# Causal mask of a 16-head attention layer: one full-height product a tile in place of two of half height

## The reference

```python
Q = (x @ Wq + bq).reshape(B, S, 16, 16)      # K, V alike
logits = jnp.einsum('bqhd,bkhd->bhqk', Q, K) * scale
causal = jnp.tril(jnp.ones((S, S), bool))
attn = jax.nn.softmax(jnp.where(causal, logits, -jnp.inf), axis=-1)
gated = attn * gate[:, None, None, :]        # gate: a small net on x
out = jnp.einsum('bhqk,bkhd->bqhd', gated, V).reshape(B, S, E) @ Wo + bo
```

## Time and profile before

| | us |
|---|---|
| median of 3 runs (3470.48 to 3481.04) | 3470.54 |
| the profiled execution | 3475.61 |
| its span, first to last instruction | 3473.8 |
| PE busy | 3212.1 (92%) |
| DVE busy | 1895.7 (55%) |
| ACT busy | 1481.7 (43%) |
| mean granted clock of PE | 0.964 |

### The profile page before, as it was taken

One profiled execution on the slowest core, in us unless ns is written; L12 is line 12 of the kernel. 1 busy time (PEld: TensorE's weight loads), 2 busy tenths in 40 slices (PEclk: granted clock), 3 DMA queues, 4 the chain that ended last, 5 costly groups with the idle time before them and its releaser, 6 DMA issues. The chain is left out here.

```text
span 3473.8 us, 50032 instructions
## 1 busy us (share of the span) xinstructions
PE 3212.1 (92%) x18306; PEld 2318.3 (67%) x18306; DVE 1895.7 (55%) x3245; ACT 1481.7 (43%) x2723; POOL 912.6 (26%) x818
## 2 busy tenths in 40 slices
PE   7996999999999999999998798998999889999998
PEld 4665756976578755986577545556465468888887
DVE  4544744775466743876465575756657433333332
ACT  3331254423543144423543465464755544444443
POOL 1213413753256512753256101001010011111111
PEclk9997999999999999999999899999999999999999
DMA  5111111111111111111111100010000130000000
GB/s 195 64 43 56 37 27 45 37 49 33 30 47 54 41 27 41 45 49 30 30 50 48 27 2 26 2 21 6 2 25 2 36 150 13 13 13 13 7 7 13
DMA packets 184276, 126.20 MB, mean 36 GB/s; under 512 B 125281, under 2 KB 164449, under 8 KB 180577
## 3 DMA queue, kind: packets, MB, share of 16 engines
q1 hardware_dynamic: 184032, 122.97, 12.4%
HBM read 105.47 MB, written 28.44 MB: 39 GB/s over the span
## 5 line engine op out<-in xcount | busy, mean ns | idle before, releaser
L1655 ACT ACTIVATE l3b_prob<-sums 128x512 f32<-128x512 f32 (+3 forms) x768 | 333.1, 494 | 204.9 <-PE sums L1588 165.8
L1904 PE MATMUL sums<-l_uhi,l_h 128*128 128x512 f32 x1024 | 405.9, 396 | 0.0
L1904 PE MATMUL sums<-l_ulo,l_h 128*128 128x512 f32 x1024 | 405.3, 396 | 0.0
L685 POOL TENSOR_TENSOR l_qrow<-l_vm,l_qst 128x512 fp32r<-128x512 f32 x256 | 355.0, 1401 | 167.8 <-ACT l_qst L679 148.9
L1025 DVE TENSOR_REDUCE l2b_mx<-sums 128x1 fp32r<-128x1024 f32 (+7 forms) x256 | 192.7, 758 | 269.4 <-PE sums L937 267.6
L962 PE MATMUL sums<-sb_nx,l_vx 128*128 128x512 f32 (+3 forms) x768 | 307.3, 510 | 2.1 <-ACT l_od L1000 2.1
L993 ACT ACTIVATE sb_nx<-sums 128x512 f32<-128x512 f32 (+3 forms) x384 | 183.7, 493 | 263.1 <-PE sums L954 257.9
L1583 PE MATMUL sums<-l_qst,l_kst 64*128 64x512 f32 (+3 forms) x768 | 277.8, 426 | 18.0 <-DMA l_qst<-l3b_peak 8.8
L1990 DVE TENSOR_TENSOR l_ulo<-l_made,l_uhi 128x512 fp32r<-128x512 f32 x128 | 90.5, 707 | 362.1 <-ACT l_uhi L1921 362.0
L679 ACT CAST l_qst<-l_vm 128x512 fp32r<-128x512 f32 x256 | 157.8, 620 | 238.2 <-DVE l_vm L672 223.6
L1566 PE MATMUL sums<-l_kst,l_qst 64*128 64x512 f32 (+3 forms) x768 | 236.9, 431 | 20.8 <-DVE l3b_low L1667 10.9
(11 more groups left out here) (273 smaller groups left out, 7806.2 us busy)
## 6 DMA issues: line engine op xcount, KB each, us to landing
l_ve<-ve SPq DMA_DIRECT2D x34, 512.0 KB, 4.0
l_oe<-oe SPq DMA_DIRECT2D x16, 1024.0 KB, 6.5
l_vm<-weights_copy SPq DMA_DIRECT2D x32, 352.0 KB, 3.3
sb_nx<-between SPq DMA_DIRECT2D x9, 1024.0 KB, 5.7
weights_copy<-h SPq DMA_DIRECT2D x2, 4096.0 KB, 25.4
l_ve<-inverse SPq DMA_DIRECT2D x32, 256.0 KB, 3.6
l_qst<-l3b_peak SPq DMA_DIRECT2D x512, 0.5 KB, 2.0
l_h<-weights_copy SPq DMA_DIRECT2D x2, 4096.0 KB, 23.4
```

Of the source, the lines that this page charges most:

```text
L685: pool.tensor_tensor(rlo[:, i % RT, :], routed[:, i % RT, :], rhi[:, i % RT, :].bitcast(F32), ALU.subtract).then_inc(s3.routed_lo, 1)
L1655: act.activation(prob[:, i % RB, j, a, 0:hi - lo], bank(m.ps, part % SCORE, 0, hi - lo), ACT.Exp, scale=SCALE1).then_inc(s.exp_ready, 1)
L1904: run(lambda out, a, x, first, last: pe.matmul(out, a, x, start=first, stop=last))
```

## The change

The two products of 64 rows that add the mask to a tile become one product of 128 rows and 128 columns, the bf16 identity times the whole mask, for maxima and score tiles alike. The constants `rowpick` and `rowmask`, their two loads and their three casts on ScalarE go, and the wait for the loads counts 14 in place of 16.

```diff
-HPART = P // 2
...
-    rowpick = sb("rowpick", [P, 2, P], BF16)
-    rowmask_qk, rowmask_kq = sb("rowmask_qk", [P, 2, P], BF16), sb("rowmask_kq", [P, 2, P], BF16)
...
-                     (w1, "w13"), (hv, "hv3"), (gv, "gv3"), (b2, "b23"), (krow, "krow3"), (given_pick, "rowpick3"),
-                     (given_mask, "rowmask3")]
+                     (w1, "w13"), (hv, "hv3"), (gv, "gv3"), (b2, "b23"), (krow, "krow3")]
...
-            act.wait_ge(ld.weights, 16 * 16)
+            act.wait_ge(ld.weights, 16 * 14)
             act.copy(select[:, :, :, :, :].rearrange("p a b r n -> p (a b r n)"), given[:, :]).then_inc(ld.select, 1)
-            act.copy(rowpick[:, :, :], given_pick[:, :, :]).then_inc(ld.select, 1)
-            act.copy(rowmask_qk[:, :, :], given_mask[:, 0, :, :]).then_inc(ld.select, 1)
-            act.copy(rowmask_kq[:, :, :], given_mask[:, 1, :, :]).then_inc(ld.select, 1)
...
                     if hi == (t + 1) * P:
-                        pe.matmul(bank(m.ps, at, hi - lo - P, hi - lo), rowpick[rows(a), 0, :], rowmask_qk[rows(a), 0, :],
-                                  start=False, stop=True, skip_group_check=True)
-                        last = pe.matmul(bank(m.ps, at, hi - lo - HPART, hi - lo), rowpick[rows(a), 1, :],
-                                         rowmask_qk[rows(a), 1, HPART:P], start=False, stop=True, skip_group_check=True)
+                        last = pe.matmul(bank(m.ps, at, hi - lo - P, hi - lo), m.ident16[:, :], m.mask_qk[:, :], start=False,
+                                         stop=True, skip_group_check=True)
...
                     if k // TPH == n:
-                        pe.matmul(bank(m.ps, part % SCORE, 0, HPART), rowpick[rows(a), 0, :], rowmask_kq[rows(a), 0, 0:HPART],
-                                  start=False, stop=True, skip_group_check=True)
-                        last = pe.matmul(bank(m.ps, part % SCORE, 0, P), rowpick[rows(a), 1, :], rowmask_kq[rows(a), 1, :],
-                                         start=False, stop=True, skip_group_check=True)
+                        last = pe.matmul(bank(m.ps, part % SCORE, 0, P), m.ident16[:, :], m.mask_kq[:, :], start=False, stop=True,
+                                         skip_group_check=True)
```

More of the change, by code:

```diff
@@ L1283, in layer3 @@
         given = own.enter_context(nc.sbuf_tensor("l3_select_given", [P, 2 * 2 * 4 * P], F32))
-        given_pick = own.enter_context(nc.sbuf_tensor("l3_pick_given", [P, 2, P], F32))
-        given_mask = own.enter_context(nc.sbuf_tensor("l3_mask_given", [P, 2, 2, P], F32))
         def load(sp):
             pairs = [(wq, "wq3"), (wk, "wk3"), (wv, "wv3"), (wo, "wo3"), (bq, "bq3"), (bk, "bk3"), (bv, "bv3"), (bo, "bo3"),
-                     (w1, "w13"), (hv, "hv3"), (gv, "gv3"), (b2, "b23"), (krow, "krow3"), (given_pick, "rowpick3"),
-                     (given_mask, "rowmask3")]
+                     (w1, "w13"), (hv, "hv3"), (gv, "gv3"), (b2, "b23"), (krow, "krow3")]
             for tile, name in pairs:
@@ L2184, in layout3 @@
     krow = np.where(out % (4 * DH1) == 2 * DH1, np.float32(-1.0), np.float32(0.0)).reshape(P, 1)
[L2185 to L2190, removed]
     return {
@@ L2197, in layout3 @@
         "b23": np.concatenate([to_all(i["L1_attn_dp_b2"]), to_all(i["L1_attn_g_b2"])], 1),
-        "select3": select.reshape(P, -1), "krow3": krow, "rowpick3": rowpick, "rowmask3": rowmask,
+        "select3": select.reshape(P, -1), "krow3": krow,
     }
```

## The result

The changed kernel takes 4080.43 us (4077.19 to 4084.56, 4 runs) against 3475.79 us for the one before (4 runs, one more than before the prediction): a ratio of 1.1737, 95% interval 1.1704 to 1.177. It is slower, as forecast, but by 605 us where 224 were forecast, and outside the range of 3515 to 3775 us.

What follows compares the result with a forecast made beforehand. PE (TensorE) was taken as the bound. Masked-tile cases added 76.4 us a block, 306 for four; less 80 of filled waits and 2 at the start, +224 on 3470.5 gave 3694.5 us, range 3515 to 3775.

Steps and rivals of the forecast that it cites:

- the price of the shape: Layer 3 attention: changing between 64-row and 128-row products costs PE 0.09 to 0.10 us each way; chance 0.62.
- the sum at full clock: Layer 3's four attention blocks: 306 us of longer masked tiles, less 80 and 2, giving +224 us.
- the upper end: Masked tile of mean width priced from L1600, with shape changes and uncovered weight load: 0.50 us; lower end 0.28.
- the 80 us of filled waits: Attention blocks: PE waits that longer work would fill, 80 us taken from room of 42 to 164.
- 32 x 0.16: Pairs with the score tile unmasked and the maxima tile masked, 32 a block: about +5.4 us a block.
- the lead-in: Opening 12 maxima tiles of an attention block: 0.33 us each becomes 1.00 per pair, +8.0 us.
- The clock falls: Rival: thinner PE work drops masked steps to 1.2 GHz, about 3890 us, or 3760 with a third of tiles; chance 0.08.
- the same sum of cases: Masked and unmasked score and maxima tiles of an attention block, counted by what runs side by side: 76.4 us a block.
- 0.19 us a tile: The low-clock rival's price: columns cost twice, 0.15 + 0.04 more on 1024 tiles, +195 us.
- the start of the layer: Start of layer 3: two DMA issues and three casts gone from the path, 1.9 us saved once.
- ACT waiting for the mask line: Sign of being right: ACT's wait on the score tiles' last mask product grows well beyond 165.8 us.

Runs made afterwards that it cites:

- fill3: Changed kernel with three extra full-height products of 512 columns in front of each masked tile; 4591.8 us, ratio 1.3118 to 1.3302.
- one_half: Kernel before with every score, maxima, mask and warming product of the attention blocks in rows 0 to 63, first head computed twice; 4097.9 us.
- group4: Changed kernel reordered: two score and two maxima tiles issued first, then up to four full-height masks in a row; 3497.7 us, ratio 1.0068.
- touch: Kernel before, half-height masks kept, plus one overwritten full-height product of 128 columns in front of each masked score tile; 3679.1 us.
- group2: Changed kernel reordered: a score tile and the other half's maxima tile issued side by side first, then their full-height masks; 3714.0 us.
- fill: Changed kernel with one extra overwritten product of 64 rows and 512 columns in front of each masked tile; 4447.5 us.
- fill_full: Changed kernel with one extra product of 128 rows and 512 columns in front of each masked tile, behind the previous mask; 4590.1 and 4689.1 us.

## Why the prediction was right and wrong

**Right: the price of the shape, and the sum at full clock.** The step that took the upper end, 0.50 us for a masked tile of mean width, is what the full-clock stretches show (0.41 us at 128 columns, 0.58 at 512), in rows alone and not only in rows and columns. The Trainium skill, TensorEngine Tiling, section Tiling Modes, Key Properties, says that a change of tiling mode drains the engine. By that rule, the trace now agrees for 64 x 128 to 128 x 128, with 0.10 us each way. By the pace of 0.62 the change's blocks, 1172.6 us with 1005 at the low clock, would take 1172.6 - 0.38 x 1005 = 791 us at full clock, 217 over the 574 before; the forecast was +224. This is worked out, not run: no kernel here has the change's program at full clock. Nor does it show each term: the 80 us of filled waits were a choice between 42 and 164, and that choice can't be read from a run in which PE is never idle, so a part of the close agreement may be luck. One term was added up wrongly (32 x 0.16 is 5.1, not 5.4), which is 1 us in all. From fill3 one gets a higher figure, 4592 less 1024 x 0.76 us for the fillers (0.04 + 0.88 in place of 0.16), some 3814 us, an upper one since the fillers also keep plain tiles apart. Up to the first score product the lead-in grew by 7.4 us (1963.2 to 1980.95 for 1972.9 to 1983.23), forecast 8.0.

**Wrong: the step "The clock falls", chance 0.08.** It is the case that came: of the 599 us in the blocks about 382 are the low clock. I had looked at PE's idle time in the earlier trace rows, 1.06 us of 8 with the clock held, and took idle time for what would let it fall. After the change PE is almost never idle (2.5 us), and the clock is at its low level for 1005 of 1173 us. The prediction also read the clock before as 1.00 from 2006 on, which holds only to the block's last steps: there it is lower again (0.77 from 2100 to 2115 us), with PE busy for 14.70 of the 15 us, a sign in the trace of before that idle time was not the whole of it:

```profile
2100.00:2115.00 15.00, 14.70 (x125) 7.55 (x123) 4.58 (x17) 9.41 (x24) 0.00 (x0) 0.77 0.25 72
```

What I should have asked of the same sum of cases is how many rows of the array are at work: 50 of its pairs, and the lone score tiles, lose the work in the other half. one_half shows that this loss, when it is complete, is enough; fill3 that dense full-height work restores the clock with all those drains in place; group4 that restoring the pairs and making fewer excursions together give nearly all of the 605 us back. In the change this loss is not complete, since unmasked pairs still run side by side, and touch shows that excursions take clock too where those pairs are kept. How the change's own fall divides between the lost pairs and the drains' empty time was not settled.

**Wrong: its price.** I had 0.19 us a tile, columns alone at half pace. Measured are 0.28 (0.78 for 0.50): the way out of the mask (0.22 for 0.16) and the weight loads are slower too, and so are L1600 and the unmasked tiles, 256 score tiles among them, which I had left out: L1600's widest products are 1035 ns long in the mean for 625. So even this rival's 3890 us was 190 short.

**Right in sign, small in size:** the start of the layer, 3.7 us for 1.9; the cast of `select` also starts 5.8 us behind the issue of its load for 7.6 before (1906.63 to 1912.39, 1913.56 to 1921.14), which I had not counted. ACT waiting for the mask line is the sign that was named, and no other engine became the bound. The room of 80 us can't be told apart from the rest any more, as PE has no idle time left.

The Trainium skill, TensorE: Matmul & The Clock Gate, Why this matters for your kernels, ties the clock to keeping TensorE busy without idle gaps. The trace of one_half differs: from 2000 to 2040 us PE is busy for 40.00 us at a granted clock of 0.50, and its blocks are at 0.51 to 0.54. Here the measurement decides: busy in time was not enough.

## What to carry to other kernels

Where products use half of the array's rows, their running side by side can be worth more than the time they share: without it the clock fell here (one_half). So ask of every edit that parts such pairs what the granted clock will be, and price everything on PE at both levels. If a full-height product must be added among half-height ones, issue the half-height ones in pairs first and the full-height ones in a row behind them (about 20 us in place of 605 here). And blocks of the same program at different granted clocks in one trace give the price of the clock with no experiment (here a pace of 0.61 to 0.63 in three kernels).

## What was not expected of the hardware

The same block can take 187 or 219 us in one launch (group2), its granted clock 0.84 or 0.67, with no other difference seen. Fillers of 64 rows (fill) and one of 128 rows a tile (fill_full) left the blocks at 0.57 to 0.64; three took them to 1.00. And a handful of full-height products of 512 columns a block (4, and 3 more for each further maxima tile of one step) with a few warming ones, put where PE waits, take 44 us of low clock from the kernel before (61 to 17 in its blocks) and 12 us from its time.
